# First two attentions of a twelve-stage network written into one block, interleaved by slots of one batch

## The reference, cut to what matters

```
x = x + _L0_attn_ref(_layernorm(x), Wq, Wk, Wv, Wp, bp)
x = x + _L0_xattn_ref(_layernorm(x), ctx_1024, ctx_1024, mask, Wq, bq, Wk, bk, Wv, bv, Wo, bo)

_L0_attn_ref:   phi_q, phi_k = elu(x @ Wq.T) + 1, elu(x @ Wk.T) + 1     # 16 heads of 16
                A = where(tril, phi_q . phi_k, 0);  num = A @ v;  den = A.sum(-1) + 1e-6
                return (num / den) @ Wp.T + bp
_L0_xattn_ref:  scores = (x @ Wq.T + bq) . (ctx @ Wk.T + bk) / 4
                attn = softmax(where(mask, scores, -1e5));  return (attn @ (ctx @ Wv.T + bv)) @ Wo.T + bo
```

## Time and profile before

| | |
|---|---|
| median of three runs | 2493.9 us (2491.03 to 2498.77) |
| profiled execution | span 2493.0 us from the first to the last instruction; what lies outside the span is not in the page, and the span is 0.9 us under the median |
| l0a | its block's first work at 13.1 us, last instruction at 139.5 us |
| l0x | first instruction 140.7 us, first scores 151.9 us, last scores from 287.1 us on, end 310.4 us |
| TensorE busy over the whole span | 89% |
| granted TensorE clock, mean | 0.944 of full |

### The profile page before, as it was taken

How to read it: one execution, slowest core, us unless ns; L and a number is a source line. 1 busy time by engine, 2 the same in 40 slices (tenths; PEclk the granted TensorE clock), 3 DMA queues, 4 the chain that set the end, 5 groups by cost and what they waited for, 6 DMA issues and landing times. The chain is left out here.

```text
span 2493.0 us, 48623 instructions
## 1 busy us (share of the span) xinstructions
PE 2221.8 (89%) x17358; PEld 1814.4 (73%) x17360; DVE 1680.9 (67%) x3260; ACT 1318.5 (53%) x3083; POOL 805.3 (32%) x1019
## 2 busy tenths in 40 slices
PE   6979799999699797989999979999779897999875
PEld 5857587887476696778888658888567686788652
DVE  4767544774666586765677646666677785888858
ACT  4558635665477663542666443333476574445335
POOL 4656402333255442100233202222211100544365
PEclk9989879999899898979999999999889999999888
DMA  3000082113400000032211430000200002877711
GB/s 113 2 1 2 1 338 83 52 52 131 147 2 2 22 2 1 2 157 115 100 52 51 163 130 1 2 1 1 102 1 1 1 1 88 229 207 214 230 29 34
DMA packets 102933, 178.37 MB, mean 72 GB/s; under 512 B 59687, under 2 KB 71591, under 8 KB 97578
## 3 DMA queue, kind: packets, MB, share of 16 engines
q1 hardware_dynamic: 85514, 135.93, 16.4%
q0 software_dynamic: 9792, 28.85, 3.6%
q10 hardware_dynamic: 7392, 10.49, 1.2%
HBM read 112.44 MB, written 62.78 MB: 70 GB/s over the span
## 5 line engine op out<-in xcount | busy, mean ns | idle before, releaser
L2356 POOL TENSOR_TENSOR l2a_Pn<-l2a_Pn,l2a_rden 128x1024 f32<-128x1024 f32 x32 | 60.0, 1897 | 288.9 <-DVE l2a_rden L2595 288.9
L1630 ACT ACTIVATE l0f_w_parts<-l0f_W 128x512 fp32r (+1 forms) x117 | 90.4, 775 | 64.8 <-PE l0f_psG L1435 50.4
L1788 DVE TENSOR_TENSOR l0f_w_parts<-l0f_W,l0f_w_parts 128x512 fp32r<-128x512 f32 (+1 forms) x117 | 99.2, 867 | 37.7 <-ACT l0f_w_parts L1630 37.5
L1630 ACT ACTIVATE l1f_w_parts<-l1f_W 128x512 fp32r (+1 forms) x117 | 90.5, 774 | 63.1 <-PE l1f_psG L1435 50.3
L4188 POOL TENSOR_TENSOR l3x_Pn<-l3x_Pn,l3x_fac 128x616 f32<-128x616 f32 (+2 forms) x96 | 70.3, 761 | 150.3 <-DVE l3x_fac L4267 140.6
L1788 DVE TENSOR_TENSOR l1f_w_parts<-l1f_W,l1f_w_parts 128x512 fp32r<-128x512 f32 (+1 forms) x117 | 99.2, 867 | 12.6 <-ACT l1f_w_parts L1630 12.2
L1488 PE MATMUL l1f_psY<-l1f_W,l1f_XT_hT 128*128 (+1 forms) x440 | 104.2, 380 | 0.8 <-ACT l1f_XT_hT L1610 0.8
L883 ACT ACTIVATE l1a_att_Pn<-l1a_att_psS,l1a_att_nmx 128x128 f32<-128x128 f32 x256 | 91.8, 418 | 1.7 <-DVE l1a_att_nmx L1002 1.7
L883 ACT ACTIVATE l0x_Pn<-l0x_psS,l0x_nmx 128x128 f32<-128x128 f32 x256 | 91.7, 418 | 0.9 <-DVE l0x_nmx L1002 0.9
L706 POOL TENSOR_TENSOR l1a_att_Pn<-l1a_att_Pn,l1a_att_rden 128x512 f32<-128x512 f32 x64 | 66.5, 1039 | 72.1 <-DVE l1a_att_rden L1009 72.1
L1488 PEld LDWEIGHTS l1f_psY<-l1f_W,l1f_XT_hT 128*128 128x128 f32 x440 | 80.3, 190 | 10.8 <-issue 1.0
(11 more groups left out here) (883 smaller groups left out, 7652.5 us busy)
## 6 DMA issues: line engine op xcount, KB each, us to landing
relative_rows<-l3x_ext SPq DMA_DIRECT2D x32, 516.0 KB, 5.9
l1f_W<-in_l1f_w SPq DMA_DIRECT2D x9, 1536.0 KB, 20.1
l0f_W<-in_l0f_w SPq DMA_DIRECT2D x8, 1536.0 KB, 26.4
cumulative_rows<-l3x_cum SPq DMA_DIRECT2D x32, 384.0 KB, 3.4
l3x_K<-keys SPq DMA_DIRECT2D x16, 512.0 KB, 5.2
l3x_rel<-relative_rows SPq DMA_DIRECT2D x32, 231.0 KB
values<-l1f_W SPq DMA_DIRECT2D x11, 512.0 KB, 5.6
l3x_V<-values SPq DMA_DIRECT2D x16, 308.0 KB
```

Of the source, the lines that this page charges most:

```text
L1630: nc.scalar.activation(w_high[i], W[:, bass.ds(act_offsets[k] + o, m)], ACT.Copy).then_inc(high_ready, 1)
L1788: nc.vector.tensor_tensor(w_low[i], W[:, bass.ds(dve_offsets[k] + o, m)], w_high[i], ALU.subtract).then_inc(low_ready, 1)
L2356: nc.gpsimd.tensor_tensor(part, part, rden[b % 2][:, 8 * u:8 * u + 8].unsqueeze(2).to_broadcast([P, 8, P]), ALU.mult)\
```

## The change

Both attentions become a `Part` each: their four engine functions are generators now, which yield the number of the slot they are about to write. `run_parts` opens one block for both, and `by_slots` merges them on each engine: l0x's slot numbers are shifted by 16 (`part.slots`), and always the program with the lowest slot goes on; where both are at the same number l0x is written first. l0x's slot i is so slot 16+i of the block. l0a's last slots (14 to 18) and l0x's first (-2 to 2) are shared ones. l0x's masks on VectorE are prepared in slots 6, 8 and 10, its head scales and GpSimd's clearing of V at the start of the block, its square roots for batches 0 to 7 (`FIRST = 8`) in slot 12 and for 8 to 15 in slot 19 (ScalarE), with the reciprocals on VectorE in slots 13 and 20. l0x keeps its `std` and `rstd` to itself, and l0a no longer computes `early_roots`.

The PSUM banks are the same for both parts (`attention_banks`: psS, psXV, psQK, psM, psN). Where l0x first writes a bank TensorE waits until l0a's last batch has been read from it (`projections_read`, `queries_read`, `scores_read`, `sums_read`, `rows_read`). psM holds l0a's sums (before: `psO`) and l0x's transposed probabilities (`psT`). The barrier between the two stages is gone, and so is their order "all of l0a, then l0x". l1a and l1x go through `run_parts` with one part each, in the same order as before.

```diff
+def by_slots(*programs):
+    todo = [[next(program) + offset, k, program, offset] for k, (program, offset) in enumerate(programs)]
+    while todo:
+        now = min(todo, key=lambda entry: (entry[0], -entry[1]))
+        slot = next(now[2], None)
+        if slot is None:
+            todo.remove(now)
+        else:
+            now[0] = slot + now[3]
+def run_parts(nc, G, *parts):
+    offsets = [0]
+    for part in parts[:-1]:
+        offsets.append(offsets[-1] + part.slots)
...
+    @block.tensor
+    def _(pe):
+        by_slots(*[(part.tensor(pe), o) for part, o in zip(parts, offsets)])
...
 transposed_attention
+    def projections_read(eng):
+        eng.wait_ge(xnT_ready, NB)
+        eng.wait_ge(v_ready, NB)
+    def scores_read(eng):
+        eng.wait_ge(pa_raw if relu2 else pa_ready, NB)
+        eng.wait_ge(pb_raw, NB)
+    def sums_read(eng):
+        eng.wait_ge(oT_ready, NB)
+        eng.wait_ge(den_ready, NB)
...
-        early_roots(nc, G, act, mv_ready, head_ready)
+        if last:
+            early_roots(nc, G, act, mv_ready, head_ready)
...
 softmax_attention, TensorE
         def transpose_x(b):
             pe.wait_ge(xn_ready, b + 1)
             if b >= 1:
                 pe.wait_ge(v_ready, b)
+            elif before:
+                before.projections_read(pe)
...
             elif 2 * b + r // 2 > 0:
                 pe.wait_ge(pt_odd, 2 * b + r // 2)
+            elif before:
+                before.sums_read(pe)
...
 softmax_attention, ScalarE
+        if before:
+            yield -4
+            act.wait_ge(before.moments_ready, FIRST)
+            nc.scalar.activation(std[:, 0:FIRST], variances(G)[:, 0:FIRST], ACT.Sqrt, ...).then_inc(first_roots, 1)
...
+            yield i
+            if before and i == 3:
+                act.wait_ge(before.moments_ready, NB)
+                nc.scalar.activation(std[:, FIRST:], variances(G)[:, FIRST:], ACT.Sqrt, ...).then_inc(std_ready, 1)
...
 softmax_attention, VectorE
+            if before and i == -3:
+                dve.wait_ge(first_roots, 1)
+                nc.vector.reciprocal(rstd[:, 0:FIRST], std[:, 0:FIRST]).then_inc(first_inverse, 1)
...
+                normalise(0)
+                normalise(1)
+            if before and i == 4:
+                dve.wait_ge(before.moments_ready, NB)
+                dve.wait_ge(std_ready, 1)
+                step.do(nc.vector.reciprocal(rstd[:, FIRST:], std[:, FIRST:]))
...
+def first_attentions(nc, G, A):
+    C = Region(nc, "l0")
+    banks = attention_banks(C)
...
+    run_parts(nc, G, *parts)
```

More of the change, by code:

```diff
@@ L153, with __init__, _, attention_banks @@
 HEAD = 12
+FIRST = 8
+class Part:
+    def __init__(self, region, loads, loaded, count):
+        self.region, self.loads, self.loaded, self.count = region, loads, loaded, count
+def by_slots(*programs):
[11 more added lines that the diff above has]
+        offsets.append(offsets[-1] + part.slots)
+    K = Region(nc, "parts")
+    block = K.block()
+    @block.sync
+    def _(sp):
+        for part in parts:
+            for dst, src, sem in part.loads:
+                sp.dma_start(dst, src).then_inc(sem, 16)
+        for part in parts:
+            sp.wait_ge(part.loaded, part.count)
+        sp.wait_ge(G.context_loaded, 16)
+    @block.gpsimd
+    def _(pool):
+        by_slots(*[(part.gpsimd(pool), o) for part, o in zip(parts, offsets)])
+    @block.tensor
+    def _(pe):
+        by_slots(*[(part.tensor(pe), o) for part, o in zip(parts, offsets)])
+    @block.scalar
+    def _(act):
+        by_slots(*[(part.scalar(act), o) for part, o in zip(parts, offsets)])
+    @block.vector
+    def _(dve):
+        by_slots(*[(part.vector(dve), o) for part, o in zip(parts, offsets)])
+    if G.ready:
+        K.close(*[part.region for part in parts[::-1]])
+    else:
+        held, G.held = G.held + [part.region for part in parts], []
+        K.close(*held[::-1])
+def attention_banks(R):
+    return {name: R.ps(name, [P, size]) for name, size in (("psS", 2048), ("psXV", 512), ("psQK", 512), ("psM", 512), ("psN", 512))}
 def early_roots(nc, G, act, mv_ready, head_ready):
@@ L269, in transposed_attention @@
     loads, loaded, NL = ([] if early else L.loads) + G.ahead, L.loaded, L.count()
-    if G.next == "l0x":
-        load_early(nc, G, "l0x", attention_loads(nc, G, A, "l0x"))
-        loads = loads + G.ahead
     G.ahead = []
@@ L304, in transposed_attention, with queries_read, rows_read @@
     s_step, p_step = R.sem("dve_step"), R.sem("pool_step")
-    block = R.block()
+    part = Part(R, loads, loaded, NL)
+    part.slots, part.moments_ready = NB, mv_ready
+    def projections_read(eng):
+        eng.wait_ge(xnT_ready, NB)
+        eng.wait_ge(v_ready, NB)
+    def queries_read(eng):
+        eng.wait_ge(qk_ready if relu2 else qk_taken, NB)
+    def scores_read(eng):
[4 more added lines that the diff above has]
+        eng.wait_ge(den_ready, NB)
+    def rows_read(eng):
+        eng.wait_ge(x_ready, NB)
+    part.projections_read, part.queries_read, part.scores_read, part.sums_read, part.rows_read = projections_read, queries_read, scores_read, sums_read, rows_read
     NV = 4
@@ L440, in _ @@
         for i in range(-2, NB + 2):
+            if i > -2:
+                yield i
             if 0 <= i < NB:
@@ L614, in _ @@
                 add_y(i - 2)
-            if i == NB + 1:
+            if last and i == NB + 1:
                 early_inverse(nc, G, dve, head_ready, inverse_ready)
@@ L618, in _, with softmax_attention @@
                 moments(i - 3)
-        dve.wait_ge(inverse_ready, 1)
+        if last:
+            dve.wait_ge(inverse_ready, 1)
         dve.wait_ge(mv_ready, NB)
-    close_stage(G, R)
-def softmax_attention(nc, G, A, tag, kind, w, normed="layer", cross=False, biased=False, out_bias=False, saved=None, ahead=()):
+    part.gpsimd, part.tensor, part.scalar, part.vector = gpsimd, tensor, scalar, vector
+    return part
+def softmax_attention(nc, G, A, tag, kind, w, normed="layer", cross=False, biased=False, out_bias=False, saved=None, ahead=(), banks=None, before=None):
     masked = kind == "masked"
@@ L676, in heads, with gpsimd @@
         return 4 * r + 2 * c
-    @block.sync
-    def _(sp):
-        for dst, src, sem in loads:
-            sp.dma_start(dst, src).then_inc(sem, 16)
-        sp.wait_ge(loaded, NL)
-    @block.gpsimd
-    def _(pool):
+    def gpsimd(pool):
         step = Step(pool, p_step)
@@ L762, in scores @@
         def scores(b):
+            if b == 0 and before:
+                before.scores_read(pe)
             for r in range(4):
@@ L800, in weigh_values @@
                 pe.wait_ge(x_ready, b)
+            elif before:
+                before.rows_read(pe)
             for c in range(DC):
```

89 lines of the change are left out of this document (55 added, 34 removed).

## The result

In the first comparison five runs of the changed kernel had a median of 2480.9 us (2478.2 to 2485.5) against 2493.9 us for five of the kernel before: ratio 0.9953, 95% interval [0.9937, 0.9968]. Two repeats with twelve runs each gave 0.9987 [0.9976, 0.9998] and 0.9969 [0.9957, 0.9981]. The first interval excludes the second, for one and the same pair of kernels. All four groups of the kernel before together (5, 28, 28 and 21 runs, 82 in all) average 2493.0 us, all three of the changed one (29 runs) 2486.7 us; two more runs of the kernel before, in a job with another kernel, were in a slow state (2654 and 2913 us at a mean clock of 0.83 and 0.73) and are left out. The difference is -6.4 us, with twice its error -8.2 to -4.5, ratio 0.9974 [0.9967, 0.9982]. That, and not 13 us, is what I explain. The change is faster; the forecast of 8.9 us less was too much.

What follows compares the result with a forecast made beforehand. TensorE was taken to bound l0a, ScalarE and TensorE in turn l0x, with a 27.6 us hole between to win in. -10.9 + 0.4 + 1.6 = -8.9 us from 2493.9 gives 2485.0 us, range 2481 to 2491.

Steps and rivals of the forecast that it cites:

- Parts 1 and 2: Shared slots 14 and 15: l0x's first mask matmul 15.4 us earlier, its first maxima on VectorE 14.5 us earlier.
- Part 3: Bank psM: l0x's first transposed probabilities wait for l0a's oT, costing 3.6 us and leaving a gain of 10.9 us.
- Part 4: Slot 16: TensorE's idle time before q again brings the low clock; full clock would gain 1.7 us more.
- Rival B: No low clock stretch in slot 16, 1.7 us better than forecast: 2483.3 us; chance 0.12.
- Part 5: Slots 17 and 18: l0a's last statistics, addition and moments precede l0x's maxima on VectorE, +0.4 us (0 to 1.0).
- Part 6: Slot 19: square root with two table loads on ScalarE delays l0x's exponentials, +1.6 us (0 to 2.9).
- rival A: New holes in slots 17 and 19 bring more low clock, 1.7 us per stretch: 2486.7 or 2488.4 us; chance 0.27.
- Part 7: l0a's steady slots: VectorE's preparation and ScalarE's first roots moved there cost 0; 9.6 us if wholly uncovered.
- Rivals C: Work inserted in l0a is not covered: +9.6 us at most, 2494.6 us, half of it 2489.8; chance 0.11.
- D: TensorE drops to 1.2 GHz through slots 14 to 16: +23.3 us, 2508.3 us; chance 0.03.
- E: A wait holds back all of l0x until l0a has ended, no overlap: 2493.9 us; chance 0.02.

Runs made afterwards that it cites:

- shift 17: The changed kernel with l0x shifted by 17 slots instead of 16, one slot of overlap less: 0.9968 of the kernel before.
- together: The changed kernel with l0x shifted by 17 slots, second inverse roots spread over VectorE's waits, 5 idle matmuls before q of batch 2: 2483.5 us, 0.9950 of before.

## Why the prediction was right or wrong

**Parts 1 and 2: right.** Mask matmuls forecast at 136.5, measured 136.2, 137.3, 136.9; maxima forecast at 138.7, measured 138.4, 139.4, 139.1. Every later shift of these two steps is l0a's own 0.7 to 1.0 us, which it has from its first scores on.

**Part 3: right.** Transposed probabilities forecast at 150.5 with `oT` as the last releaser; measured 148.8, 151.1 and 152.2, each 0.1 us behind `oT`'s end. The exponentials of batch 1 were forecast 10.9 us earlier and measured 11.0 on average (151.8 against 162.8); that the average fits so well is luck, since the three profiles have 12.9, 10.6 and 9.5. The 3.6 us of the bank: without the wait (shift 17, low stretch) the distance from batch to batch is 9.5, with it 12.1 to 13.6: 2.6 to 4.1 us. With the idle time filled and the full clock it is 8.5 (together) against 10.9: 2.4 us.

**Part 4: the step that failed, in two ways.** I read one profile's low stretch as a fixed property of the place. The same idle time of 3.0 us ended at the full clock in one of three profiles and at the low one in two (in one of eight and seven, with the shifted kernels and those with other roots). And 1.7 us was no good price: it was 0.3 in the kernel before, where ScalarE's exponentials bound the slot, and in the changed one it is 1.2 to 2.7, since q runs low too and l0a's last weighing stands behind v. Rival B was this profile's case: forecast 1.7 us ahead of 151.7, measured 149.93. The Trainium skill, "TensorE: Matmul & The Clock Gate", section "What's actually happening", has the throttled state as the default that activity releases. The changed kernel with idle matmuls agrees (1.00), but its first profile without them had the full clock behind 3.02 us of idle time as well. The kernel before with them shows that a hole's low clock need not reach the end.

**Part 5: right in place, smaller.** +0.16 us (9.02 against 8.86), forecast 0.4. **Part 6: right.** +1.70 (10.69 against 9.00), forecast 1.6, and 0.1 more one batch later. The drain that the Trainium skill, "ScalarE: Activation LUTs", section "What ACT_TABLE_LOAD costs", adds to a load does not show: 1.30 us from the second load's start to the exponential's, and none between the copy and that load. In the third profile the late exponentials opened a low stretch before q of batch 5 (+1.55): rival A, once in three.

**Part 7: right.** l0a's slots stayed at 6.85 us (scores at 92.70, 99.55 and 106.40 in the first profile), and neither the preparation nor the first roots cost anything. Rivals C, D and E did not occur.

**The sum.** At batch 4's exponentials the mean gain is 8.5 us (181.1 against 189.7; 10.9, 8.6 and 6.1 in the three profiles), forecast 8.9. At l0f's start it is 7.1 (304.0 against 311.2), because one of the two profiles of before had a lucky end of l0x. In the runs it is 6.4, error 0.9. "Everything from l0f on some 9 us earlier and otherwise alike" was wrong as a test: two executions of one program differ by 3 to 5 us in l0f alone. The 2480.9 of the first comparison stands 4 us under my 2485.0 and the 2487.0 median of all 29 runs 2 us over it; neither side is a step of mine. What part of the 2.5 us between -8.9 and -6.4 is the price of part 4 and what is chance of five profiles stays open.

## What to carry to other kernels

When two pipelines are merged, gain and loss sit at the shared buffers: follow the one bank that both use, and offset the second pipeline until its first use falls behind the first one's last read; one slot of overlap less was no loss. The barrier and the preparation were worth under 2 us, the work placed under the drain nearly all. Before explaining a difference under 10 us in a program of 2500, profile both versions twice and compare stage by stage.
